# A fused attention and expert kernel: four low weight halves formed on TensorE and rounded on ScalarE, zeros on TensorE at the start, and another order of VectorE's work before the first routed block

## What is computed

```python
# x: 4 batches of 512 rows x 512, ctx: 4 x 512 x 128
x = x + attn(ctx, layernorm(x))      # added to the residual
x = x + ffn(layernorm(x))

def attn(h, adj, Wq, Wk, g):
    sim = (h @ Wq.T) @ (h @ Wk.T).T / (sqrt(32) * 4)          # 512 x 512
    thr = top_k(sim, 153)[..., -1:]                            # per row
    A = sigmoid(sim) * (sim >= thr)
    return (1 - sigmoid(g)) * adj + sigmoid(g) * (A + A.T) / 2

def ffn(x):                                                    # 2048 tokens
    top-2 of 8 experts by softmax(x @ router.T), weights renormalised
    out  = sum_e combine_e * (silu(x @ gate_e) * (x @ up_e)) @ down_e       # 352 wide
    out += (silu(x @ s_gate + b1) * (x @ s_up + b2)) @ s_down + b3          # 704 wide
```

## Time and profile before

| | us |
|---|---|
| median of 3 runs (lowest to highest) | 520.33 (520.3 to 521.56) |
| the profiled execution, its own time | 520.39 |
| its span in the profile | 518.5 |
| PE busy | 452.1 (87%) |
| DVE busy | 337.9 (65%) |
| ACT busy | 238.8 (46%) |
| POOL busy | 166.3 (32%) |

### The profile page before, as it was taken

How to read it: one execution, slowest core, us unless ns; L and a number is a source line. 1 busy time by engine, 2 the same in 40 slices (tenths; PEclk the granted TensorE clock), 3 DMA queues, 4 the chain that set the end, 5 groups by cost and what they waited for, 6 DMA issues and landing times.

```text
span 518.5 us, 9429 instructions
## 1 busy us (share of the span) xinstructions
PE 452.1 (87%) x2794; PEld 255.0 (49%) x2795; DVE 337.9 (65%) x961; ACT 238.8 (46%) x427; POOL 166.3 (32%) x214
## 2 busy tenths in 40 slices
PE   5204699999999999999958999999999999999960
PEld 2103344545454545454425666666666666666630
DVE  3999999999999999648854555555556433333310
ACT  5991666259725972445442444444444322222220
POOL 2000400053004300440132454555555444444431
PEclk9755779999999999999987999999999999999995
DMA  8800630129002700265286678777777544445541
GB/s 270 248 1 35 210 102 1 48 93 205 2 23 100 123 0 23 105 121 114 88 224 196 162 182 200 181 189 189 183 186 172 85 82 83 85 85 86 86 81 22
DMA packets 39005, 60.54 MB, mean 117 GB/s; under 512 B 8233, under 2 KB 18729, under 8 KB 38962
## 3 DMA queue, kind: packets, MB, share of 16 engines
q0 software_dynamic: 10384, 23.38, 26.0%
q1 hardware_dynamic: 26514, 36.61, 22.4%
q10 hardware_dynamic: 2064, 0.02, 0.2%
HBM read 37.68 MB, written 22.30 MB: 116 GB/s over the span
## 4 chain that ended last, share of the span: by engine, by line
PE 67%; DVE 18%; ACT 5%; issue 3%; DMA 3%; POOL 1%; SPq 1%; DVEq 0%; POOLq 0%; ACTq 0%
PE bank L935 5%; PE bank L937 5%; PE bank L936 5%; PE bank L1095 4%; PE bank L1094 4%; PE bank L1093 4%; PE bank L1069 4%; PE bank L1073 4%; PE bank L1071 4%; PE bank L1070 4%; PE bank L1072 4%; PE bank L1074 4%; PE bank L1055 3%; PE bank L1082 2%; PE bank L882 2%
## 5 line engine op out<-in xcount | busy, mean ns | idle before, releaser
L535 POOL DMA_INDIRECT out_dram<-xb,sidx x35 | 55.9, 1597 | 84.7 <-ACT xb L819 77.9
L935 PE MATMUL bank<-xT,W 128*128 128x512 f16 x176 | 67.9, 386 | 0.6 <-DVE sgt L1409 0.6
L936 PE MATMUL bank<-xT,W 128*128 128x512 f16 x176 | 67.8, 385 | 0.0
L937 PE MATMUL bank<-xT,W 128*128 128x512 f16 x176 | 67.7, 385 | 0.0
L1538 DVE TENSOR_TENSOR hS<-bank,hS 128x384 f16<-128x384 f32 x35 | 19.5, 557 | 72.2 <-ACT hS L811 72.2
L805 ACT ACTIVATE sgt<-bank 128x352 f32<-128x352 f32 x35 | 16.2, 464 | 92.7 <-PE bank L1074 92.7
L819 ACT ACTIVATE xb<-bank,wcol 128x512 f32<-128x512 f32 x35 | 24.0, 687 | 54.8 <-PE bank L1095 54.8
L1533 DVE SCALAR_TENSOR_TENSOR xb<-bank,sgt 128x352 f32<-128x352 f32 x35 | 18.3, 524 | 41.4 <-ACT sgt L805 40.4
L1069 PE MATMUL bank<-W,xT 128*128 x140 | 44.3, 316 | 0.9 <-DVE W L1151 0.8
L1071 PE MATMUL bank<-W,xT 128*128 x140 | 44.3, 317 | 0.0
L1073 PE MATMUL bank<-W,xT 128*128 x140 | 44.3, 317 | 0.0
(11 more groups left out here) (245 smaller groups left out, 1001.8 us busy)
## 6 DMA issues: line engine op xcount, KB each, us to landing
xn_dram<-W SPq DMA_DIRECT2D x16, 256.0 KB, 3.2
out_dram<-W POOLq DMA_DIRECT2D x12, 256.0 KB, 6.0
stage<-L_ffn_down_w_in SPq DMA_DIRECT2D x12, 256.0 KB
sim<-L_ffn_down_w_in SPq DMA_DIRECT2D x12, 256.0 KB
stage<-L_ffn_gate_w_in SPq DMA_DIRECT2D x16, 176.0 KB
stage<-L_ffn_up_w_in SPq DMA_DIRECT2D x16, 176.0 KB
sim<-L_ffn_gate_w_in SPq DMA_DIRECT2D x16, 176.0 KB
sim<-L_ffn_up_w_in SPq DMA_DIRECT2D x16, 176.0 KB
```

Source lines behind the costliest of these rows:

```text
L935: pe.matmul(o, wh, xT[:, 0, c, :], start=(c == 0), stop=False)
L936: pe.matmul(o, wh, xT[:, 1, c, :], start=False, stop=False)
L937: last = pe.matmul(o, wl, xT[:, 0, c, :], start=False, stop=(c == KD - 1))
```

## The change

- **Zeros.** As soon as DVE has cleared `ylast`, PE multiplies zeros into bank 7: four matmuls of 512 columns at the very start, one behind the weight product, two behind the context transposes, two behind the projection.
- **Four low halves on PE.** The low halves of shared pieces 4 to 7 leave DVE. Each is formed in two parts of 352 columns: PE multiplies the fp32 copy by the identity and, in the same bank, the high half by the identity times -1/64 (a new constant, written by POOL); ACT rounds the result into place (`round_low`, eight of them). Parts 0 to 3 stand on PE behind the router's transposes, parts 4 to 7 behind batch 0's transposes of the masked scores and ahead of the scores of batch 1. ACT's eight roundings stand behind the projection copy of batch 1.
- **Batch 0.** On ACT the high halves 4 to 7, the sums and the squares come later, between the counts and behind the fourth; the masked sigmoids come ahead of `apply_ln`, and the copy of batch 1's context ahead of the six high halves of the shared down weights. On DVE the layer norm's small operations move from the third and fourth pass to places behind the second and fourth tile of `threshold_below`.
- **Routing.** One high half more (piece 7) stands on ACT ahead of the last `sh_hi`. On DVE two low halves come ahead of part 5 of the shared hidden layer instead of three behind it, then one, then piece 7; the six low halves 8 to 13 now all stand behind the first `routed_x`.
- **End.** In the second step of the last pair, `routed_down` of the block before runs in the middle of `routed_up`.

```diff
-FIRST_AT = [0, 2, 2, 2, 1, 0, 0]
-FIRST_LOW = [0, 0, 2, 2, 0, 3]
-SECOND_AT = [2, 2, 2, 1]
+FIRST_AT = [0, 2, 2, 2, 1, 1]
+FIRST_LOW = [0, 0, 2, 2, 0, 2]
+SECOND_AT = [2, 2, 2, 0]
...
+        def round_low(f):
+            act.wait_ge(s_lowps, f + 1)
+            lo = UNITS[PE_LOWS[f // 2]][2] + (f % 2) * (SI // 2)
+            act.activation(W[:, lo:lo + SI // 2], bank[4 + f % 4][:, 0:SI // 2], ACT.Copy, scale=WS).then_inc(s_wloA, 1)
...
+            for t in range(TB):
+                sig_scores(0, t)
             apply_ln(0)
+            context_T(1)
             split_some(SC)
-            for t in range(TB):
-                sig_scores(0, t)
-            context_T(1)
             proj(1)
+            for f in range(LOW_PARTS):
+                round_low(f)
...
+        def keep_on(n):
+            for _ in range(n):
+                pe.matmul(bank[7][:, :], zeros16[:, 0:P], zeros16[:, 0:512], start=True, stop=True)
+
+        def form_low(f):
...
+            pe.matmul(o, ident[:, :], staged(n)[0][:, at:at + SI // 2], start=True, stop=False)
+            pe.matmul(o, minus16[:, :], W[:, hi:hi + SI // 2], start=False, stop=True).then_inc(s_lowps, 1)
...
             for c in range(KD):
+                if between and c == KD // 2:
+                    between()
...
-        for n in range(4):
+        for n in range(KD - 1):
             weight_lo(n)
...
-                if b == 0:
-                    weight_lo(4 + t)
+                if b == 0 and t == 0:
+                    weight_lo(3)
...
-            if b == 0 and it == 3:
-                gamma_parts()
-                layer_norm_x(0)
...
+            if b == 0:
+                gamma_parts()
+                layer_norm_x(0)
             link(dve.tensor_scalar(dif[:, 0, :], hi_[:, 1, :], -1.0, float(KTH), ALU.mult, ALU.add))
...
+        later_weights(1)
+        shared_lo(last_b, SC - 1)
+        later_weights(AHEAD)
...
-        later_weights(4)
         routed_x(0, 0)
-        later_weights(sum(SECOND_AT) - 4)
+        later_weights(sum(SECOND_AT))
...
-        step(j + 1, (j + 1) // 2, (j + 1) % 2, fetch=j + 4 < BLOCKS)
+        step(j + 1, (j + 1) // 2, (j + 1) % 2, fetch=j + 4 < BLOCKS, ends=True)
```

More of the change, by code:

```diff
@@ L99, with lows_done @@
 LAST = LATE + PER_EXPERT
[L102 to L104 removed]
+PE_LOWS = range(KD, 2 * KD)
+LOW_PARTS = 2 * len(PE_LOWS)
+def lows_done(n):
+    return n - len(PE_LOWS)
+FIRST_AT = [0, 2, 2, 2, 1, 1]
+FIRST_LOW = [0, 0, 2, 2, 0, 2]
+SECOND_AT = [2, 2, 2, 0]
 BLOCK_UNITS = 2
[L106 to L108 removed]
+AHEAD = sum(FIRST_AT) - PER_EXPERT
+assert sum(FIRST_LOW) + 1 == PER_EXPERT
+assert AHEAD + sum(SECOND_AT) + BLOCK_UNITS * HEAD_BLOCKS == len(UNITS) - SECOND
+assert all(AHEAD + sum(SECOND_AT) + BLOCK_UNITS * min(4 * r - 1, HEAD_BLOCKS) >= PER_EXPERT * r for r in range(1, E))
 def place_of(n):
@@ L407, in load_ranked @@
             if last >= RANKED:
[L408 removed]
+                sp.wait_ge(s_wloD, lows_done(last + 1))
             place, loaded = staged(n)
@@ L553, in _, with step @@
         gather(2, 0)
-        def step(j, m, p, fetch=True, alone=False):
+        def step(j, m, p, fetch=True, alone=False, ends=False):
             if fetch:
@@ L706, in _ @@
         early_hi(2)
+        scores(0, 0)
         early_hi(3)
-        for t in range(TB):
+        for t in range(1, TB):
             scores(0, t)
-            early_hi(4 + t)
-        for t in range(TB):
-            x_total(t)
+        early_hi(4)
+        early_hi(5)
+        early_hi(6)
         count(0, 0)
-        x_mean()
-        x_square(0)
-        x_square(1)
+        early_hi(7)
         def first_batch():
+            x_total(0)
             count(0, 1)
-            x_square(2)
-            x_square(3)
+            x_total(1)
+            x_total(2)
             count(0, 2)
+            x_total(3)
+            x_mean()
+            count(0, 3)
+            for t in range(TB):
+                x_square(t)
             small_inputs()
-            count(0, 3)
-            apply_ln(0)
-            split_some(SC)
             for t in range(TB):
                 sig_scores(0, t)
+            apply_ln(0)
             context_T(1)
+            split_some(SC)
             proj(1)
+            for f in range(LOW_PARTS):
+                round_low(f)
         def later_batch(b):
@@ L1005, in _ @@
         transpose_router()
+        for f in range(4):
+            form_low(f)
         for b in range(NB):
@@ L1018, in _ @@
                 transpose_A(b, t)
+            if b == 0:
+                for f in range(4, LOW_PARTS):
+                    form_low(f)
             if b:
@@ L1056, in routed_x, with routed_up @@
             last.then_inc(s_x2ps, 1)
-        def routed_up(j, p, at):
+        def routed_up(j, p, at, between=None):
             pe.wait_ge(s_x2, j + 1)
@@ L1108, in step @@
             if not isinstance(j, int):
-                pe.wait_ge(s_wloD, len(UNITS))
+                pe.wait_ge(s_wloD, lows_done(len(UNITS)))
             elif j == 0:
-                pe.wait_ge(s_wloD, SECOND)
+                pe.wait_ge(s_wloD, lows_done(SECOND))
             elif j % 4 == 0 and j < HEAD_BLOCKS:
-                pe.wait_ge(s_wloD, SECOND + j // 4 * PER_EXPERT)
+                pe.wait_ge(s_wloD, lows_done(SECOND + j // 4 * PER_EXPERT))
+            if ends:
+                routed_up(j, p, at, lambda: routed_down(j - 1, 1 - p, where(j - 1)))
+                return
             routed_up(j, p, at)
```

58 lines of the change are left out of this document (37 added, 21 removed).

## The result

The changed kernel takes 515.54 us (median of 4, 514.56 to 516.29) against 520.32 us (4 runs, 519.66 to 521.56) for the kernel before: a ratio of 0.9903, 95% interval [0.9877, 0.9930]. The profiled execution took 514.56 us with a span of 512.8; before it was 520.39 and 518.5. The forecast was 512.7 us, its range 510.9 to 516.4.

A forecast was written before the change was run, and what follows sets the result against it. PE was taken as the bound from 80 us on, DVE's chain with ACT before; gains of 0.7 (start), 6.5 (routed blocks) and 0.45 (last pair) sum to 7.65, from 520.39 to 512.7 us, range 510.9 to 516.4.

The forecast's parts named there:

- rival (a): First routed block: the clock falls in the routing gap, `routed_up` takes 6.4 us, gain there 4.2, total 515.0; chance 0.18.
- Parts 1 to 3: Start, batch 0: aggregation 4.1 us earlier at 14.2, threshold 3.6, but DVE waits 2.3 for high half 8; mask 1.2 earlier.
- the 0.7 us of the sum: Whole start up to batch 1: 1.2 - 0.3, less some 0.2 for a late clock rise; ends -1.5 and 1.3.
- Part 4: PE ahead of batch 1's scores: four low parts cost 3.6 us, between 2.9 and 5.9; DVE loses 0.3.
- Part 5: First routed block: PE's gap 1.3 us instead of 5.9, `routed_up` in 3.6; gain 6.5 us, ends 4.3 and 7.0.
- the 7.0: First routed block: last shared down products cover PE to 277.7 against 284.7 before, ahead of 0.5 taken off for DVE.
- (b): Routing: loads of down pieces 12 and 13 take 5.5 us, gain there 4.6, total 514.6; chance 0.10.
- (d): Routing: DVE's second copy hangs on piece 13's load; landing at 282.5 makes the kernel 1.6 us slower, 522; chance 0.03.
- (c): Start: zeros don't raise the clock (2.4 us there) or PE's low parts run low (cost 3); 513.6 to 515; chance 0.11.
- Part 6: Last pair: `routed_down` of 33 ends 1.8 us earlier, scatter 33 starts at 500.1 instead of 500.55; gain 0.45, ends 0 and 0.6.
- ACT's copy by 497.9: Last pair: ACT copies block 33's result by 497.9 us, its `routed_down` having ended 1.8 earlier than 499.0.
- the 1.9 us of block 34's opened hidden path: Last pair: block 34's hidden path, no longer covered by products, adds 1.9 us, but scatter 34 waits for scatter 33 anyway.

The follow-up runs named there:

- the second four: The changed kernel run once more, unaltered, on the chip of the other three comparisons: 514.70 us (4 runs, 513.85 to 515.84), ratio 0.9895.

## Why the prediction was right where it was, and wrong where it was not

**The whole.** The time is 2.8 us above the forecast, outside its likeliest 511 to 514 and inside its range. The profiled execution accounts for 1.8 of it: the start gave 1.1 less than forecast and the end 0.8 less, while the routed blocks gave what was forecast. The other 1.0 lies between that execution and the median of the four, of which no trace tells; the second four have their median at 514.70. The upper end of the range was made for rival (a) at a price of 2.3 us. The measured time lies below it, but what brought it there is mostly the start and the end, so that the range held is in part luck.

**Parts 1 to 3, the start: the steps hold, their head start differs.** The clock rose with the zeros, and the step from the aggregation to the threshold's reading takes 20.98 us in the changed kernel against 20.65, that is 0.3 more where the forecast had 0.5. DVE's wait for high half 8 was forecast at 2.3 and is 2.61, and it starts low half 8 4.16 us behind the threshold's reading (forecast 4.0). What failed is the first step, the aggregation at 14.2: it was at 15.79 and 14.51 in the two profiles. 0.5 us of the difference between the two is the landing of the first weight, which one profile of before can't bound. The rest stands between the weight and the scores: in the first profile PE's projection still took the low level's 2.07 us, and in the second ACT's copy of it stood behind high half 1, whose data landed only at 7.5 us; with the copy moved ahead the aggregation came at 14.11. The forecast counted PE and the clock there, but not ACT's order. Since everything behind it hangs on it in a fixed distance, the mask moved with it, to 43.92 and 42.65, forecast 42.3. In place of the 0.7 us of the sum the start cost 0.4 in the one profile and gave 0.9 in the other.

**Part 4, low parts on PE: right.** 3.65 us for four, forecast 3.6, one at 1.4 and three at the high level. The 0.3 that DVE was to lose did not come: it goes on behind POOL's power, at 57.02, which is 13.10 us behind the mask, as before (56.62 and 43.52).

**Part 5, the routed blocks: right.** 6.4 us, forecast 6.5. (One mark of the sum is 0.3 too late: the last shared down products of before are done not at 284.7 but at 284.43, where the next group starts, so by its own terms the 7.0 is 6.7 and the 6.5 is 6.2.) PE's stall for the low half was 0.59 (forecast 0.7), its gap 1.42 (1.3), the address 0.51 (0.8), and `routed_up` ran at the high level. The bound behind it was DVE at 277.9, inside the 276.9 to 278.7 of the forecast. Rivals (b) and (d) did not come: the two down pieces were issued by 271.44 and in use at 274.21, 2.8 us later, and the second copy was at 277.28. Nor did (c), whose prices were off by its own terms: 2.4 instead of 4.1 in part 1 gives 514.4, and 3 instead of 0.3 in part 4 gives 515.4, not 513.6 to 515. **Rival (a)**, at 0.18, was under-weighted: it came in four of nine profiled executions with this order. But its price was put too high. The forecast gave it a `routed_up` of 6.4 us; in the trace shown above the clock came back after twelve of 24 products, which costs 1.7 us, of which 1.1 is left behind DVE, and by scatter 32 between 0.4 and 1.2. The Trainium skill (TensorE: Matmul & The Clock Gate, section "HAM oscillation") says that waits between bursts of matmuls take the clock down again. The waits of its example are longer than these gaps; with these, the runs agree in four cases and not in five.

**Part 6, the last pair: wrong in sign.** Forecast 0.45 gained, ends 0 and 0.6; measured 0.5 lost. Three steps failed. "ACT's copy by 497.9" took it that ACT was free once the products were done. On ACT that copy stands behind the Silu of block 34, which needs all of `routed_up`, now lengthened by the nine products moved into it: 2.2 us of waiting. And the 1.9 us of block 34's opened hidden path were called covered by scatter 33; PE stood still for 1.11 and 1.26 us there, in the profiled execution the clock fell, and six of the nine last products ran at 0.43, so that scatter 34 ended up behind PE. (In the second profile of the changed kernel it stayed high, and the loss was 0.3.) Moving the copy ahead of the Silu takes the loss away, but gives no gain, and that is the third step: the landing of scatter 32 was counted with 5.06 us, the time of scatter 33's. Where the next scatter waits for it, it takes 5.60 and 5.52, which alone leaves nothing of the 0.45.

**The interplay of the parts** was no step of the forecast. The routing order gives 5.2 us on the kernel before, but 3.2 on top of the new start (516.82 to 513.62), because the new start by itself already shortens the same wait by 1.2 to 1.7 us and lets the clock return sooner. The forecast added the parts up as if each were alone; here that did no harm, since it took part 5 from the trace of before, which has neither.

## What to carry to other kernels

Before counting an earlier product as a gain, read what stands ahead of its consumer on the consumer's own engine: ACT's copy behind a Silu cost more here (0.5 us) than the move could bring. Where several engines share a bound, an engine that gets ahead is no gain; in the two profiles where PE then stood idle for 3.4 us, the clock made it a loss of 1.7. The wait of 6 us that was cut to 1.4 brought back the clock as well, but only in five of nine profiles: count it as two cases with prices of their own, and take more than one profile.

## What the runs showed that was not expected

- After the same two gaps on PE (1.42 and about 0.5 us) the granted clock fell in four profiled executions and stayed high in five; `routed_hT` of block 0 comes 0.8 to 1.5 us later for it, scatter 32 0.4 to 1.2.
- One issue on SP's queue takes 1.23 to 1.38 us instead of 0.38 in three of three profiles with the old start and in neither of the new start with the old routing; with it goes 1.2 to 1.7 us of PE's wait 200 us behind the edit.
- POOL's all-reduce of `bad` runs 2.7 to 2.9 us behind its input in all ten profiles with the new start, and 0.1 us behind it in the four with the old one. In the kernel with three high halves first it ran at 40.17, though POOL shows no other work behind 34.4:

```profile
40.17 0.38 POOL L522 PARTITION_ALL_REDUCE bad<-bad  x1 [5.77 <-issue]
```

Its input was ready at 37.3. These 2.8 us became DVE's next wait once the one for the high half was gone; what they consist of was not tried.
